# Two-layer block on one core: dt u of the selective scans moves from PSUM to SBUF, four products move to GpSimd, and the experts get four PSUM buffers and three Newton steps

## The reference, cut to what matters

```
# scan, per batch: 512 channels, 16 states, 1024 tokens
dt = softplus(...);  A = -exp(A_log);  u = silu(conv(...))
h  = h * exp(dt * A) + (dt * u) * B          # one recurrence per channel and state
y  = sum over states of h * C;  y = (y + u * D_skip) * silu(z);  out = y @ W_out
# experts: for each token the best and the second best of 8
eo_i = relu(x_i @ W1[e_i] + b1[e_i]) @ W2[e_i] + b2[e_i];  x_2 = x + 0.5 * eo_1
g = silu(layer_norm(x + w_1 * eo_1 + w_2 * eo_2) * gamma + beta)
x = x + out * g
```

## Time and profile before

| | us |
|---|---|
| median of 3 runs (2278.11 to 2285.85) | 2283.58 |
| the profiled execution, its own time | 2274.25 |
| span of the profile | 2272.5 |
| scans, first to last (256 steps) | 948.3 to 1889.9 |
| first expert pass | 1889.9 to 2068.2 |
| second expert pass | 2068.2 to 2272.5 |

### The profile page before, as it was taken

One profiled execution on the slowest core, in us unless ns is written; L12 is line 12 of the kernel. 1 busy time (PEld: TensorE's weight loads), 2 busy tenths in 40 slices (PEclk: granted clock), 3 DMA queues, 4 the chain that ended last, 5 costly groups with the idle time before them and its releaser, 6 DMA issues. The chain is left out here.

```text
span 2272.5 us, 25527 instructions
## 1 busy us (share of the span) xinstructions
PE 1933.3 (85%) x7956; PEld 1056.0 (46%) x7956; DVE 1708.3 (75%) x2363; ACT 1256.4 (55%) x1646; POOL 1224.6 (54%) x651
## 2 busy tenths in 40 slices
PE   5799889979996998889889998999886678998984
PEld 3335534643563364333325332433242236887873
DVE  4984688378737824699999999999989994334887
ACT  3873585277427822667654665466644434665663
POOL 2601531071118010388788899989976673223664
PEclk9899899989998999899999999999989989999997
DMA  6510550074016304688888888989899983233442
GB/s 186 121 38 0 160 119 19 1 201 95 1 47 158 74 38 71 142 293 295 284 296 297 294 282 294 316 295 297 271 298 381 331 322 111 98 98 111 134 139 78
DMA packets 177319, 402.62 MB, mean 177 GB/s; under 512 B 48175, under 2 KB 77105, under 8 KB 176035
## 3 DMA queue, kind: packets, MB, share of 16 engines
q1 hardware_dynamic: 165154, 371.09, 52.2%
q0 software_dynamic: 12032, 29.90, 4.6%
HBM read 356.30 MB, written 45.51 MB: 177 GB/s over the span
## 5 line engine op out<-in xcount | busy, mean ns | idle before, releaser
L1224 POOL TENSOR_TENSOR late<-late,rows 128x1024 f32<-128x1024 f32 x256 | 603.1, 2365 | 142.2 <-DVE late L1701 137.7
L1874 PE MATMUL m_Q<-late,ident_m 128*128 128x512 f32 x1024 | 531.5, 651 | 144.5 <-POOL late L1224 108.0
L1701 DVE TENSOR_TENSOR_SCAN late<-m_Q,late 128x1024 f32<-128x1024 f32 x256 | 586.3, 2290 | 40.2 <-ACT m_Q L1410 11.5
L1410 ACT ACTIVATE m_Q<-late,acol 128x1024 f32<-128x1024 f32 x256 | 286.1, 1117 | 358.7 <-DVE late L1701 357.0
L1874 PEld LDWEIGHTS m_Q<-late,ident_m 128*128 128x128 f32 x1024 | 196.6, 204 | 445.7 <-POOL late L1224 248.4
L1694 DVE TENSOR_TENSOR late<-m_Q,rows 128x1024 f32<-128x1024 f32 x256 | 307.0, 1199 | 11.6 <-DMA rows<-bc_s 11.2
L489 DVE SCALAR_TENSOR_TENSOR early<-early,work 128x1024 f32<-128x1024 f32 x128 | 155.9, 1218 | 32.7 <-ACT early L625 30.5
L1933 PE MATMUL m_Q<-late 128*128 128x128 f32 x1248 | 158.4, 281 | 8.0 <-issue 0.9
L1933 PEld LDWEIGHTS m_Q<-late 128*128 128x128 f32 x1248 | 147.8, 194 | 33.1 <-issue 31.3
L313 POOL TENSOR_TENSOR qkh<-early,qkh 128x1024 bf16<-128x1024 f32 x12 | 25.5, 2128 | 250.8 <-ACT qkh L593 250.8
L633 ACT ACTIVATE early<-early 128x1024 f32<-128x1024 f32 x128 | 134.8, 1053 | 42.6 <-DVE early L494 41.2
(11 more groups left out here) (234 smaller groups left out, 3386.8 us busy)
## 6 DMA issues: line engine op xcount, KB each, us to landing
rows<-bc_s SPq DMA_DIRECT2D x512, 512.0 KB, 5.6
rows<-st_s SPq DMA_DIRECT2D x64, 384.0 KB, 5.6
st_s<-qkh SPq DMA_DIRECT2D x16, 768.0 KB, 5.8
r_s<-late SPq DMA_DIRECT2D x39, 256.0 KB, 2.0
rows<-st_s SPq DMA_DIRECT2D x64, 128.0 KB, 6.3
xin<-in_x SPq DMA_DIRECT2D x4, 1024.0 KB, 8.8
xres<-in_x SPq DMA_DIRECT2D x4, 1024.0 KB, 5.5
mx_s<-s SPq DMA_DIRECT2D x4, 1024.0 KB, 4.5
```

The lines of the kernel that those rows point to most:

```text
L1224: nc.gpsimd.tensor_tensor(pr[:, n % NH, :], h[:, n % NH, :], cb[:, n % NCB, :], ALU.mult).then_inc(pr_ok, 1)
L1410: A(dA[:, :], dt[:, (b * KI + m) % 2, :], ACT.Exp, scale=acol[:, m, i % NS:i % NS + 1]).then_inc(dA_ok, 1)
L1701: v_.tensor_tensor_scan(h[:, n % NH, :], dA[:, :], dB[:, n % 2, :], 0.0, ALU.mult, ALU.add).then_inc(h_ok, 1)
L1874: ins = mm(half(Y, c), ident[:, :], half(pr[:, n % NH, :], c), start=False, stop=(n % NS == NS - 1), skip_group_check=True)
```

## The change

- dA gets two PSUM buffers (`m_Q0` and `m_Q1`), so `decay` waits for the scan of step n-2 and not of n-1.
- du moves out of PSUM into an SBUF tensor `m_du` with two buffers. POOL's `drive` writes it directly; ACT's copy is gone (15 operations).
- dB gets three buffers. In batch 0 the product of state 5 of each tile (four in all, `ON_POOL`) is done by POOL, three steps ahead, and left out of DVE's program.
- The second layer of the experts gets four PSUM buffers; PE waits for the tile of four earlier.
- Three Newton steps in place of four.
- gamma and beta are loaded after the last scan, into space of the scans, and `normalise` waits for them.

```diff
-NBB, NCB, NH, NU = 3, 4, 3, KI + 1
+NBB, NCB, NU = 3, 4, KI + 1
+NH, NPR, NDB = 3, 3, 3
+ON_POOL = [b * STEPS + m * NS + s for b, m, s in ([(0, m, 5) for m in range(KI)])]
-        dus = sb("dus", [P, L])
+        du = sb("m_du", [P, 2, L])
-        pT1, _, pM2, pT2 = Q
-        dA, du, _, Y = (q[:, :, :].rearrange("p a b -> p (a b)") for q in Q)
+        pT1, pM2a, pM2b, pT2 = Q
+        product = lambda q: (pM2a, pM2b)[q // 2 % 2][:, q % 2, 0:D]
+        *dA, _, Y = (q[:, :, :].rearrange("p a b -> p (a b)") for q in Q)
...
+        def wait_product(eng, n):
+            if n in ON_POOL:
+                eng.wait_ge(dBp_ok, ON_POOL.index(n) + 1)
+            else:
+                eng.wait_ge(dB_ok, n + 1 - sum(j < n for j in ON_POOL))
...
+                sp.wait_ge(h_ok, B * STEPS)
+                for i, n in enumerate(("ln_gamma", "ln_beta")):
+                    sp.dma_start(gamma[:, i, :], g[n].rearrange("(a n) -> a n", a=1).to_broadcast([P, D])).then_inc(gb_in, 16)
...
-                    pool.wait_ge(du_ok, t)
-                    nc.gpsimd.tensor_tensor(dus[:, :], dt[:, t % 2, :], u[:, t % NU, :], ALU.mult).then_inc(dus_ok, 1)
+                    if t >= 2:
+                        pool.wait_ge(h_ok, (t - 1) * NS)
+                    nc.gpsimd.tensor_tensor(du[:, t % 2, :], dt[:, t % 2, :], u[:, t % NU, :], ALU.mult).then_inc(du_ok, 1)
+
+                def times_b(n):
+                    pool.wait_ge(b_in[n % NBB], 16 * (n // NBB) + 16)
+                    pool.wait_ge(du_ok, n // NS + 1)
+                    pool.wait_ge(h_ok, n - NDB + 1)
+                    nc.gpsimd.tensor_tensor(dB[:, n % NDB, :], du[:, n // NS % 2, :], bb[:, n % NBB, :], ALU.mult).then_inc(dBp_ok, 1)
...
                         times_c(b, i)
+                        if b * STEPS + i + NDB in ON_POOL:
+                            times_b(b * STEPS + i + NDB)
...
-                    if n:
-                        ac.wait_ge(h_ok, n)
-                    A(dA[:, :], dt[:, (b * KI + m) % 2, :], ACT.Exp, scale=acol[:, m, i % NS:i % NS + 1]).then_inc(dA_ok, 1)
-
-                def drive_out(t):
-                    ac.wait_ge(dus_ok, t)
-                    ac.wait_ge(dB_ok, t * NS)
-                    A(du[:, :], dus[:, :], ACT.Identity).then_inc(du_ok, 1)
+                    if n >= 2:
+                        ac.wait_ge(h_ok, n - 1)
+                    A(dA[n % 2], dt[:, (b * KI + m) % 2, :], ACT.Exp, scale=acol[:, m, i % NS:i % NS + 1]).then_inc(dA_ok, 1)
...
-                    v_.tensor_tensor(dB[:, n % 2, :], du[:, :], bb[:, n % NBB, :], ALU.mult).then_inc(dB_ok, 1)
+                    v_.tensor_tensor(dB[:, n % NDB, :], du[:, t % 2, :], bb[:, n % NBB, :], ALU.mult).then_inc(dB_ok, 1)
...
-                    v_.tensor_tensor_scan(h[:, n % NH, :], dA[:, :], dB[:, n % 2, :], 0.0, ALU.mult, ALU.add).then_inc(h_ok, 1)
+                    v_.tensor_tensor_scan(h[:, n % NH, :], dA[n % 2], dB[:, n % NDB, :], 0.0, ALU.mult, ALU.add).then_inc(h_ok, 1)
...
-                    for _ in range(4):
+                    for _ in range(3):
...
+                        dv.wait_ge(gb_in, 32)
...
-                    if q >= 2:
-                        pe.wait_ge(m2c, q - 1)
+                    if q >= 4:
+                        pe.wait_ge(m2c, q - 3)
```

More of the change, by code:

```diff
@@ L991, in phase_me @@
         xi4 = rows[:, 0:KI * (DC - 1 + L)].rearrange("p (m t) -> p m t", m=KI)
-        late = sb("late", [P, 10 * L])
+        late = sb("late", [P, 11 * L])
         def part(of, at, shape, dt=F32):
@@ L1012, in phase_me @@
         h = part(late, 0, [NH, L])
-        pr = part(late, 3 * L, [NH, L])
-        dB = part(late, 6 * L, [2, L])
-        dt = part(late, 8 * L, [2, L])
+        pr = part(late, NH * L, [NPR, L])
+        dB = part(late, (NH + NPR) * L, [NDB, L])
+        dt = part(late, 9 * L, [2, L])
         w_bc, w_dt, acol, taps, vecs, one, ident = (g[n] for n in ("w_bc", "w_dt", "acol", "taps", "vecs", "one", "ident_m"))
         w_out = sb("mw_out", [P, KI, D])
-        dus = sb("dus", [P, L])
+        du = sb("m_du", [P, 2, L])
         xi = sb("m_xi", [P, 2, DC - 1 + L])
@@ L1031, in phase_me @@
         ext = sb("ext", [P, 2, NTILE, 4], I32)
-        gamma = sb("gamma", [P, 2, D])
+        gamma = part(late, 8 * L, [2, D])
         b1c = sb("e_b1c", [P, E * HE // P])
@@ L1065, in phase_me @@
         rest = tile([NR - 2, 2 * D]); out1 = tile([3, 2 * D])
[L1066 removed]
+        first = part(late, 9 * L, [2, 2 * D])
         row = lambda n: first[:, n % NR, :] if n % NR < 2 else rest[:, n % NR - 2, :]
         xsT = tile([2, KD * P]); ws = tile([2, KD * HE]); hT = tile([2, HE])
[L1069 removed]
+        st = sb("st_e", [P, 2, GROUP, 6]); mv = sb("mv_e", [P, 2, GROUP, 2]); rs = sb("rs_e", [P, 4, GROUP]); spare = rs[:, 3, 0:1]
         Q = [ctx.enter_context(nc.psum_tensor(f"m_Q{i}", [P, 2, CH], F32)) for i in range(4)]
[L1072 to L1073 removed]
+        pT1, pM2a, pM2b, pT2 = Q
+        product = lambda q: (pM2a, pM2b)[q // 2 % 2][:, q % 2, 0:D]
+        *dA, _, Y = (q[:, :, :].rearrange("p a b -> p (a b)") for q in Q)
         X = [Q[2][:, i, :] for i in range(2)]
@@ L1718, in _ @@
                     scan(n)
-                    if n + 1 < B * STEPS:
+                    if n + 1 < B * STEPS and n + 1 not in ON_POOL:
                         times_b(n + 1)
@@ L1739, in boost @@
                     m = out1[:, n % 3, D:]
-                    v_.tensor_tensor(m, pM2[:, n % 2, 0:D], b2[:, bass.ds(e * D, D)], ALU.add).then_inc(m2c, 1)
+                    v_.tensor_tensor(m, product(n), b2[:, bass.ds(e * D, D)], ALU.add).then_inc(m2c, 1)
                     dv.wait_ge(m2c, n + 1)
@@ L1761, in fuse @@
                     dst = f[:, n % NF, :]
-                    v_.scalar_tensor_tensor(dst, pM2[:, (NTILE + n) % 2, 0:D], w, row(n)[:, D:], ALU.mult, ALU.add).then_inc(m2c, 1)
+                    v_.scalar_tensor_tensor(dst, product(NTILE + n), w, row(n)[:, D:], ALU.mult, ALU.add).then_inc(m2c, 1)
                     dv.wait_ge(m2c, NTILE + n + 1)
@@ L1873, in add_state @@
                     for c in range(NC_):
-                        ins = mm(half(Y, c), ident[:, :], half(pr[:, n % NH, :], c),
+                        ins = mm(half(Y, c), ident[:, :], half(pr[:, n % NPR, :], c),
                                  start=False, stop=(n % NS == NS - 1), skip_group_check=True)
```

35 lines of the change are left out of this document (14 added, 21 removed).

## The result

The changed kernel takes 2471.93 us (median of 4 runs, 2468.10 to 2472.43) against 2280.85 (4 runs, 2276.27 to 2285.85): ratio 1.0845, 95% interval 1.0827 to 1.0862. It is slower, and slower than the range: 2397 was forecast, at most 2455. The profiled execution took 2471.69 us, with a span of 2470.0 us and a mean granted TensorE clock of 0.917 (0.948 before).

The account below looks back on a forecast made before the run. VectorE was taken to bound the scans, GpSimd after the change. Scans +119.5 us and experts -7 made +112.5, put on the median of 2283.58: 2397 us, range from a little under 2340 to 2455.

Parts of the forecast that it names:

- Experts: Expert passes: three Newton steps shorten VectorE's chain, four PSUM buffers bring nothing; -7 us, between -8 and -2.
- GpSimd becomes the bound: Scans: GpSimd's work plus holds exceeds VectorE's in batches 0 to 2; +135.5 us over four batches, +119.5 after a deduction.
- 1.0 us a product: Scans: time GpSimd stands still for each VectorE product from two SBUF tensors, in nearly each step.
- two steps ahead: Scans: with three h buffers VectorE can be this far ahead, then stands until `times_c` has read the oldest.
- If GpSimd is in flight, VectorE waits for its end: Scans: VectorE's product then goes first and GpSimd's next product stands behind it, again 1.0 us.
- +27.2 forecast: Batch 0: GpSimd's 191.9 us, four moved products and 60 holds make 261.3 us against 234.1.
- forecast +3: Batch 3: GpSimd reaches 234.4 us, VectorE bounds at 236.9, and GpSimd's lag at its start remains.
- I take a quarter of them, 16 products, 16 us: Scans: products meeting the 64 indirect DMAs cost nothing if the issue is not held; 16 us deducted.
- the sign that it is too low: Indirect DMAs in the profile: their mean of 1002 ns would have grown if their issue is held up too.
- The whole length and more: Rival, scans: each product costs GpSimd 1.22 us and indirect DMAs hide none; some +186 us, 2470; chance 0.09.
- 2387 + 9.3: Whole kernel: forecast for the profiled execution, plus its distance under the median of the runs; given as 2397 us.
- the small price: Rival, scans: GpSimd loses only 0.4 to 0.7 us a product, partly buffered; together +7 to +55 us; chance 0.05.

Follow-up runs that it names:

- du_sbuf: Kernel before with only du moved to a double SBUF tensor, ACT's copy gone: 2504.71 against 2312.44 us, ratio 1.0826.
- du_back: Changed kernel with du read from PSUM again, so one dA buffer, all else kept: 2312.97 against 2312.44 us, ratio 0.9998.
- micro: Separate test kernel, nothing of the reference computed: VectorE's two-SBUF product asked at varied delays beside GpSimd's back-to-back SBUF products; one run, 676.6 us.
- drained: Changed kernel with a tiny memset and a wait for it behind each indirect DMA of batches 1 and 2: 2467.51 against 2316.42 us, ratio 1.0671.
- micro2: Separate test kernel, nothing of the reference computed: GpSimd issues an indirect DMA, then six products, while VectorE asks at varied delays; one run, 743.0 us.

## Why the prediction was wrong

**Right.** VectorE bounds the scans, and two SBUF inputs make its product and GpSimd's products exclude each other, in both directions: all of the earlier trace rows carried over, du_sbuf and du_back show that it is this move and no other, micro shows it alone. The product itself costs no more (1199 ns where it is free). The four products are worth nothing or less, the two dA buffers 5.7 us of scans at most. Experts: -7 forecast, -6.6 and -6.8 measured.

**Step 1 that failed: "GpSimd becomes the bound".** I added up GpSimd's busy time and 1.0 us a product, and let VectorE run two steps ahead to keep GpSimd fed. "If GpSimd is in flight, VectorE waits for its end" stands in the prediction, but has no term in its sum. But VectorE isn't ahead: it stands in its own product for the end of GpSimd's operation, 2.1 us each time GpSimd has one more operation in a step. The room of a step is 3.49 - 3.15 = 0.34 us for GpSimd, and GpSimd can't save it up, since each `times_c` needs the recurrence just ended. So it idles 130 us in the scans (31.7 to 33.3 us a batch, by the same groups batch by batch) and VectorE still loses. The price that counts is VectorE's 2.1 us by the number of extra operations: in batch 0, where the DMAs play no part, GpSimd runs 23 operations other than its 64 `times_c` (87 in the window), and 23 x 2.1 less the 4.8 us of moved products is 43.5 us, against +40.2 measured and +27.2 forecast. In batch 3 it is 9 x 2.1 = 19 (two of the nine are indirect DMAs of the experts), measured +13.1, forecast +3. That is an estimate behind the event; in the trace it is 25 longer products in batch 0 with 47.0 us. That estimate was possible from the earlier trace rows: 2.28 us for 0.17 was a turn of VectorE's, and the sum used that row only for GpSimd's side.

**Step 2: "I take a quarter of them, 16 products, 16 us".** The indirect DMAs were credited with hiding 16 us. They cost. Without them batches 1 and 2 of the change are 99 us shorter, and the scans of the kernel before 6 us, so some 93 us of the 201 are theirs. Of these the passing over of VectorE's product explains at least the 33 us that drained recovers; their held issue (1.81 instead of 1.00 us, 64 times, 52 us of GpSimd's time) is a candidate for the rest, which wasn't separated. The prediction named a grown mean of that row as the sign that it is too low; it grew by 81%.

**The size of the hold.** 1.0 us was taken from the earlier trace rows; in a plain step it is 0.8: 3.15 - 2.37 in the kernel, 0.79 in micro. It depends on who starts how much later. In all these rows it is what the first operation has left when the other asks, less some 0.14 us: 1.2 - 0.26 - 0.14 = 0.8 in the kernel, 2.34 - 0.10 - 0.14 = 2.10 for VectorE in micro, and 2.35 - 0.16 - 0.14 = 2.05 in the earlier trace rows (2.03 measured), where two operations followed each other, so that dividing by two gave too much for one.

**The rival that gave the right number.** "The whole length and more" said 2470, and 2472 was measured, but by 1.22 us a product on a full GpSimd. Neither is so: the hold is shorter than the product, and GpSimd idles. That the two numbers agree is luck. The Trainium skill (SBUF — State Buffer, "Who interferes with whom") says that whoever issues first keeps the pair of SBUF ports that the two share for the whole instruction; micro agrees for the instruction under way. I had read its length as 1.22 us a product on GpSimd; the same rule with VectorE as the loser gives what is left of a GpSimd product of 2.37 us, and that is the 2.1 us that decided. It has no word of an engine passing several times, which micro2 shows. The same section infers that a product of VectorE doesn't hinder the generation of descriptors; here the issue of an indirect DMA, whose indices and entries stand in SBUF, takes 1.57 to 1.72 us beside one and 0.96 alone. Which part of the issue stands wasn't measured.

**The range** took its upper end from GpSimd's sum. With VectorE's side added it would have had to reach beyond 2470. Two slips of arithmetic decide nothing: 2387 + 9.3 is 2396 and not 2397, and the small price's 12 to 35 us a batch, less 7 for the experts, come to some +21 to +60 and not +7 to +55.

## What to carry to other kernels

Where VectorE and GpSimd work side by side on SBUF, keep one input of VectorE's operations in PSUM; freeing a PSUM buffer by moving that input made scans of 942 us 201 us longer here. When two engines exclude each other, don't add up busy times per stage: take one step, see who asks while the other is under way, and price each extra operation at what the asking engine stands, on the engine that bounds. And if an indirect DMA has to stand in GpSimd's program among such products, a tiny operation and a wait for it behind the DMA give VectorE its turn back (33 us here).

## What the runs showed of the hardware that was not expected

- Behind the issue of an indirect DMA, GpSimd's back-to-back operations pass a waiting VectorE product: all six of them in micro2 (15.17 us); in the kernel the product gets in one or two operations later than its turn (4.35 to 6.68 us). Without the DMA it gets in at the end of the one under way. Of the requests in the change that came into an operation directly behind an indirect DMA, with another operation directly behind that (within 0.1 us), 37 of 37 were passed; of those into any other operation with one directly behind it, 0 of 37. In drained 1 request was passed at all, in batch 3, behind an indirect DMA of the experts that has no memset behind it. Why the tiny operation with its wait ends this wasn't found out.
- The order of start decides what is lost: VectorE first by 0.26 us costs GpSimd 0.8 us; GpSimd first costs VectorE up to 2.1 us, and GpSimd's next operation about 1 us as well.
- The duration of an instruction in the profile includes the time that it stands for the other engine (a 1.2 us product listed with 15.17). A busy share near 1 doesn't say that the engine works.
